# A decoder layer on one core: the attention phase's batch loop as a loop in hardware, and the head norm's means at another place

## The chip, the core and the metric

The kernel runs on one core of a Trainium2 chip. The metric is the device time of one execution in microseconds, median of three runs. A core has five instruction streams: TensorE (PE, with its weight loads PEld), VectorE (DVE), ScalarE (ACT), GpSimd (POOL) and SyncE (SP), which here issues the DMAs. They run in parallel and meet at semaphores only.

## The reference, cut to what matters

One decoder layer on x of 8 x 512 x 512, in three parts, each followed by a layer norm over the last axis without weights.

```python
x = _layernorm(x + attention(x, ...))        # the phase that the change is in
x = _layernorm(x + retention(x, ctx, ...))
x = _layernorm(x + coupling_network(x, ...))

# attention: 16 heads of 32
kv = _ln(x, kvn_w, kvn_b) @ kv_w + kv_b
q = _ln(x, qn_w, qn_b) @ q_w + q_b
q, k = _rotary(q, x, rh_w, rh_b), _rotary(k, x, rh_w, rh_b)
qn, kn = _ln(q, ln_w, ln_b), _ln(k, ln_w, ln_b)      # the head norm, over 32 elements
attn = softmax(einsum('bhqd,bhkd->bhqk', qn, kn) / sqrt(32))
out = einsum('bhqk,bhkd->bhqd', attn, v) @ out_w + out_b
```

## The kernel before

The three parts run one behind the other (`attention_phase`, `retention_phase`, `coupling_phase`). In the attention phase the work is cut into 32 units U = 4 b + g: b is one of 8 batch rows (B = 8), g one of four groups of four heads (G = 4, HG = 4). Each engine has its own list of instructions, written out by a function `unit(b, g, left, more)`: sixteen steps i = 0 to 15, and at each step the pieces that fall due there. `left` says how many units follow (4 for "enough"), `more` whether there is a batch row b + 2.

A unit works on several units' data at once. In unit U the engines do:

- for U: the key-side scores (`key_scores`, L929), their exponentials (`exps`, L796), the weighing of v (`weigh`, L939), the inverse of the sums, and at i = 15 the normalisation (`normalise`, L550); the high and low halves of its result are taken in the next unit (`attn_hi`, L802, `attn_low`, L554).
- for U + 1: the row scores (`query_scores`, L911) in three banks (NB = 3), so that product i waits for exponential i - 3; the row maxima (`row_max`, L526); their exponentials for the sums (`sum_exps`, L775); at the end the maxima are turned (`transpose_max`, L918), saved (`save_max`, L788) and spread (`spread_max`, L532).
- for U + 2: the head norm, for the key side (s = 0) and the query side (s = 1): mean on VectorE (`head_mean`, L497 and L499), subtraction on GpSimd (`centre`, L362), square on ScalarE (`square`, L759), variance on VectorE (`head_var`, L507 and L510), power and multiplications on GpSimd (`head_norm`, L368 to L377), transposes on TensorE (`turn_heads`, L897), halves, and 24 DMAs into `stack`.
- for U + 3: the projection (`project`, L886 to L888), its save by two additions (`save_qkv`, L489 and L491), and the rotation on GpSimd (`rotate`, L344 to L354), whose semaphore `turned` the mean waits for.
- with g = 0 also the output projection of the batch row before (L953 to L955), transposes of the next row's x, and only one bank for the projection.

The order on an engine is the order in which `unit` writes its pieces; an engine takes its instructions in that order. Tables at the head of the file set the steps: `QS_DONE`, `KS_DONE` and `PROJECT_DONE` say how many products are done after step i, `SQUARE_AT = (1, 2)` when ScalarE squares sides 0 and 1, `VAR_AFTER = (2, 3)` when VectorE takes the variances. Semaphores only count up, so that a wait names a number that grows with U. `steps` counts an engine's waits on its own operations. The class `Steps` has `loop` and `end`, and `in_registers` writes out the additions for a value that isn't a constant; neither is used before the change. `run` writes out all 32 units one behind the other for each engine.

Of the kernel before, what the change touches and what calls it, by code (L numbers as in the profile page):

```python
# [19 lines left out]
B, S, D = 8, 512, 512  # L20
T = S // P
K = D // P
H, HD = 16, 32
G = 4
HG = H // G
GQ = HG * HD
EPS = 1e-5

KS_DONE = tuple(min(4 * (i + 1) // 3, T * HG) for i in range(16))
QS_DONE = tuple(min(max(4 * (i - 1) // 3, 0), T * HG) for i in range(16))  # L30
# [4 lines left out]
Z_AT, Z_HIGH_AT, Z_LOW_AFTER = (12, 12, 13, 13), (13, 13, 14, 14), (13, 13, 14, 14)  # L35
MAX_AT, SAVE_MAX_AT = 14, 14
X_NORM_AT, STATS_AFTER, FINAL_AFTER, SHIFT_AFTER = (6, 7, 8, 9), (5, 7), 9, 4
VAR_AFTER, SQUARE_AT = (2, 3), (1, 2)
TURN_HIGH_AT, TURN_LOW_AFTER = ((9, 12), (9, 11)), ((10, 13), (10, 12))
INVERT_AFTER, INVERSE_AT, INVERSE_SAVE_AT, ATTN_HIGH_AT, ATTN_LOW_AFTER = 6, 11, 12, 0, 0  # L40
NB = 3
# [10 lines left out]
def in_registers(eng, *values):  # L52

    for value in values:
        if not isinstance(value, int):
            eng.compute_val(value)
# [78 lines left out]
def attention_phase(nc, x, x1, w, ctx_in, w_next, ret):  # L137
# [6 lines left out]
    with ctx:  # L144
# [87 lines left out]
        dve_step, pool_step = sem("dve_step"), sem("pool_step")  # L232
# [14 lines left out]

        block = ctx.enter_context(nc.Block())

        def run(unit):  # L250

            for b in range(B):
                for g in range(G):
                    unit(b, g, 4 if b < B - 1 else G - 1 - g, b + 2 < B)

        @block.sync
        def _(sp):
# [46 lines left out]
            for U in range(2):  # L304
                for s in range(2):
                    regroup_side(U, U, s)
            run(unit)
            sp.wait_ge(qkv_done, T * G * B)
            for m in (0, 2, 1):
                sp.dma_start(ret.raw[m], w_next[("Wk", "Wq", "Wv")[m]].rearrange("(k p) n -> p k n", p=P)).then_inc(ret.load_w, 16)  # L310
# [8 lines left out]
        def _(pool):  # L319
# [98 lines left out]
            x_rstd(1)  # L418
            for s in range(2):
                rotate(2, s)  # L420
            run(unit)
            pool.wait_ge(ret.xvar_done, 1)
            nc.gpsimd.tensor_tensor(ret.rstd[:, :], ret.rstd[:, :], minus_half[:, 0:T], ALU.pow).then_inc(ret.xrstd_done, 1)

# [1 line left out]
        def _(dve):  # L426
# [10 lines left out]
            def x_stats(b, t):  # L437

                if t == 0:
                    dve.wait_ge(x_in, 16 * (b + 1))  # L440
                nc.vector.bn_stats(stats[:, t, :], z[:, t, :])
                nc.vector.scalar_tensor_tensor(scratch[:, :], z[:, t, :], 1.0, rh_w[:, :], ALU.mult, ALU.mult,
                                               accum_out=per_step[:, t:t + 1]).then_inc(dve_step, 1)
                dve.wait_ge(dve_step, steps.next())

            def x_moments(b):

# [138 lines left out]
            def unit(b, g, left, more):  # L586
                U = G * b + g
                for i in range(T * HG):
                    if left == 0 and i == R_STATS_AT:
                        next_stats()  # L590
                    if left == 0 and i == R_NORM_AT:
                        next_norm()
                    if left == 0 and i in SPLIT_AT:
                        next_lower(*SPLITS[SPLIT_AT.index(i)])
                    if left >= 2 and i == 0:
                        for s in range(0 if U == 0 else 1, 2):
                            head_mean(U + 2, s)
                    if left >= 1:
                        for m in within(QS_DONE, i):
                            row_max(U + 1, m)  # L600
                    if left >= 3 and i in SAVE_AFTER[g > 0]:
                        t = SAVE_AFTER[g > 0].index(i)
                        save_qkv(U + 3, (g + 3) % G, t, bank_t[0 if g == 0 else t % 2])
                    if i == ATTN_LOW_AFTER and counts(U):
                        attn_low(U - 1, (g - 1) % G)
                    for s in range(2):
                        if left >= 2 and i == VAR_AFTER[s]:
                            head_var(U + 2, s, g == 2)
                    for s in range(2):
                        if left >= 2 and i == TURN_LOW_AFTER[g > 0][s]:  # L610
                            turn_low(U + 2, s, bank_t[s])
                    if g >= 2 and more and i in STATS_AFTER:
                        x_stats(b + 2, 2 * (g - 2) + STATS_AFTER.index(i))
                    if g == 3 and more and i == FINAL_AFTER:
                        x_final(b + 2)
                    if g == 0 and left == 4 and i == SHIFT_AFTER:
                        x_shift(b + 1)
                    for t in range(T):
                        if g == 0 and counts(b) and i == ADD_AFTER[t]:
                            add_out(b - 1, t, bank_t[1])  # L620
                        if g == 0 and left == 4 and i == Z_LOW_AFTER[t]:
                            z_low(b + 1, t)
                    if i == INVERT_AFTER:
                        invert(U, g % 2)
                    if i == SAVE_MAX_AT and left >= 3:
                        head_mean(U + 3, 0)
                    if i == SAVE_MAX_AT and left >= 1:
                        spread_max(U + 1, (g + 1) % 2)
                    if i == T * HG - 1:
                        normalise(U)  # L630
# [98 lines left out]
            spread_max(0, 0)  # L729
            for s in range(2):  # L730
                turn_low(1, s, bank_t[s])
            run(unit)
            attn_low(G * B - 1, G - 1)
            next_lower(*SPLITS[-2])
            for t in range(T):
# [4 lines left out]
        def _(act):  # L740
# [122 lines left out]
            save_max(0, 0)  # L863
            for s in range(2):
                turn_high(1, s, bank_t[s])
            run(unit)
            attn_hi(G * B - 1, G - 1)
            for m, half in SPLITS[-2:]:
                next_higher(m, half)
# [2 lines left out]
        def _(pe):  # L872
# [225 lines left out]
            for s in range(2):  # L1098
                pe.wait_ge(qkv_saved, T * 2 + 3 + s)
                turn_heads(1, s, bank_t[s])  # L1100
            run(unit)
            pe.wait_ge(attnT_done, G * B)
            for t in range(T):
                project_out_part(t, G - 1)
# [1066 lines left out]
```

## Time and profile before

| | |
|---|---|
| time, median of 3 runs | 2055.28 us (2052.32 to 2055.53) |
| the profiled execution's own time | 2052.32 us |
| its span, first to last instruction | 2050.4 us |
| instructions in it | 26478 |
| TensorE / weight loads busy | 1777.7 / 1329.2 us |
| VectorE / ScalarE / GpSimd busy | 1455.5 / 1258.5 / 861.0 us |
| mean granted TensorE clock | 0.946 of full |
| attention phase | the first 1097 us or so |

The span is what the trace covers; the own time is what is comparable with other runs. Busy times of engines overlap each other. A busy TensorE isn't TensorE at its peak, since its products are pipelined.

### The profile page before, as it was taken

How to read it: one execution, taken by the hardware profiler on the slowest of the kernel's cores; microseconds unless marked ns; L12 is line 12 of the kernel's file. 1: busy time of each engine (PE TensorE's matmuls, PEld its weight loads, DVE VectorE, ACT ScalarE, POOL GpSimd, SP SyncE). 2: the span in 40 equal slices, each digit the busy share in tenths (PEclk: the TensorE clock that was granted, in tenths of full speed). 3: DMA queues.
4: the chain of work that ended last, by engine and by line, in shares of the span. 5: the costliest groups of instructions: out<-in, count | busy, mean ns of one | idle time of the engine just before them, and what ended most of it. 6: DMA issues, size and time to landing. Idle time of an engine off the chain costs nothing. (4 is left out here: it accounts for less than half of the span.)

```text
span 2050.4 us, 26478 instructions
## 1 busy us (share of the span) xinstructions
PE 1777.7 (87%) x8648; PEld 1329.2 (65%) x8648; DVE 1455.5 (71%) x2915; ACT 1258.5 (61%) x2674; POOL 861.0 (42%) x802
## 2 busy tenths in 40 slices
PE   6788888888888888888888999999986999999972
PEld 5556566666566665666536878787775777777751
DVE  7768677686776867767655767676653678888876
ACT  3388777886868868688693232322323667777764
POOL 3677678676876768768521222222220000000000
PEclk9799999999999999999889999999997999999996
DMA  4222232322323223222252101111121011111111
GB/s 151 58 77 62 57 98 62 94 61 62 93 62 98 57 61 94 62 78 57 69 168 108 62 36 48 54 55 57 62 88 41 21 42 62 62 62 62 42 41 62
DMA packets 86184, 141.06 MB, mean 69 GB/s; under 512 B 16544, under 2 KB 19616, under 8 KB 86048
## 3 DMA queue, kind: packets, MB, share of 16 engines
q1 hardware_dynamic: 86048, 139.37, 22.0%
q8 instruction: 70, 1.15, 0.2%
q14 instruction: 66, 0.54, 0.1%
HBM read 63.82 MB, written 25.17 MB: 43 GB/s over the span
## 5 line engine op out<-in xcount | busy, mean ns | idle before, releaser
L526 DVE TENSOR_REDUCE a_neg_max<-a_max 128x1 fp32r<-128x512 f32 x512 | 340.4, 684 | 175.4 <-PE a_max L911 173.3
L796 ACT ACTIVATE a_probs<-a_exp 128x512 f32<-128x512 f32 x512 | 294.2, 606 | 209.6 <-PE a_exp L929 208.7
L775 ACT ACTIVATE a_max<-a_max,a_neg_max 128x512 f32<-128x512 f32 x512 | 347.1, 689 | 15.3 <-DVE a_neg_max L526 13.5
L911 PE MATMUL a_max<-a_stack 96*128 96x512 f32 x512 | 224.7, 463 | 92.3 <-ACT a_max L775 84.6
L368 POOL TENSOR_TENSOR a_rstd<-a_rstd,a_minus_half 128x16 f32<-128x16 f32 x64 | 186.0, 2906 | 90.4 <-DVE a_rstd L510 90.3
L911 PEld LDWEIGHTS a_max<-a_stack 96*128 96x128 f32 x512 | 99.1, 197 | 190.7 <-ACT a_max L775 141.0
L886 PE MATMUL a_t<-a_w_hi,a_zT_hi 128*128 128x384 f32 x500 | 181.5, 363 | 32.8 <-DVE a_v L491 23.0
L1717 POOL TENSOR_TENSOR f_yrstd<-f_yrstd,f_minus_half 128x4 f32<-128x4 f32 x8 | 11.0, 1376 | 472.0 <-DVE f_yrstd L1736 472.0
L929 PE MATMUL a_exp<-a_stack 100*128 100x512 f32 x512 | 192.0, 416 | 9.9 <-ACT a_probs L796 6.5
L887 PE MATMUL a_t<-a_w_lo,a_zT_hi 128*128 128x384 f32 x500 | 173.4, 347 | 0.0
L888 PE MATMUL a_t<-a_w_hi,a_zT_lo 128*128 128x384 f32 x500 | 173.2, 346 | 0.0
L939 PE MATMUL a_o<-a_probs,a_v 128*32 128x512 f32 x1024 | 151.1, 665 | 0.0
L886 PEld LDWEIGHTS a_t<-a_w_hi,a_zT_hi 128*128 128x128 f32 x500 | 99.3, 199 | 48.1 <-DVE a_v L491 31.3
L1449 ACT ACTIVATE r_kq_hi<-r_part 128x512 fp32r<-128x512 f32 x64 | 36.9, 625 | 147.3 <-POOL r_part L1316 147.3
L1996 PE MATMUL f_l<-f_h_hi,f_w_hi 128*128 128x512 f32 x240 | 100.6, 419 | 25.2 <-DVE f_h_lo L1726 24.6
L775 ACT ACTIVATION_READ_ACCUMULATOR a_max<-a_max,a_neg_max 128x1 f32 x512 | 120.4, 235 | 0.0
L929 PEld LDWEIGHTS a_exp<-a_stack 100*128 100x128 f32 x512 | 100.6, 197 | 28.6 <-ACT a_probs L796 15.7
L1996 PE MATMUL f_w<-f_xT_hi,f_w_hi 128*128 128x512 f32 x256 | 104.4, 408 | 7.4 <-DVE f_xT_lo L1726 7.4
L362 POOL TENSOR_TENSOR a_n<-a_n,a_mean 128x512 f32<-128x512 f32 x64 | 73.7, 1156 | 76.5 <-DVE a_mean L499 75.3
L887 PEld LDWEIGHTS a_t<-a_w_lo,a_zT_hi 128*128 128x128 f32 x500 | 99.5, 199 | 8.1
L1322 POOL TENSOR_TENSOR r_yrstd<-r_yrstd,r_minus_half 128x2 f32<-128x2 f32 x16 | 11.2, 697 | 222.8 <-DVE r_yrstd L1417 222.8
L1726 DVE TENSOR_TENSOR f_h_lo<-f_full,f_h_hi 128x512 fp32r<-128x512 f32 x104 | 70.4, 688 | 43.1 <-ACT f_h_hi L1899 42.0
(286 smaller groups left out, 4919.7 us busy)
## 6 DMA issues: line engine op xcount, KB each, us to landing
a_stack<-a_nT_hi SPq DMA_DIRECT2D x512, 64.0 KB, 2.0
a_stack<-a_nT_lo SPq DMA_DIRECT2D x256, 64.0 KB, 2.0
a_z<-x SPq DMA_DIRECT2D x8, 1024.0 KB, 7.9
a_y<-x SPq DMA_DIRECT2D x8, 1024.0 KB, 5.7
r_xn<-x SPq DMA_DIRECT2D x8, 1024.0 KB, 5.6
r_cn<-ctx SPq DMA_DIRECT2D x8, 1024.0 KB, 7.9
x<-r_xn SPq DMA_DIRECT2D x16, 512.0 KB, 2.8
f_xn<-x SPq DMA_DIRECT2D x8, 1024.0 KB, 5.6
```

What stands on the lines that cost most here:

```text
L362: nc.gpsimd.tensor_tensor(n[:, c], n[:, c], wide(mean[:, c]), ALU.subtract).then_inc(centred, 1)
L368: nc.gpsimd.tensor_tensor(rstd[:, c], rstd[:, c], minus_half[:, :], ALU.pow).then_inc(pool_step, 1)
L526: nc.vector.tensor_reduce(neg_max[:, t, ROW + h:ROW + h + 1].bitcast(F32R), bank_max[i % NB][:, :], AX_X, ALU.max, negate=True).then_inc(m ...
L775: nc.scalar.activation(bank_max[i % NB][:, :], bank_max[i % NB][:, :], ACT.Exp, bias=neg_max[:, t, ROW + h:ROW + h + 1], accum_out=sums[:, ...
L796: nc.scalar.activation(probs[:, kt % 2, h, :], bank_exp[i % 2][:, :], ACT.Exp).then_inc(exp_done, 1)
L886: mm(bank, zT_hi[:, k, at], w_hi[:, k, g, :], start=k == 0, stop=False)
L887: mm(bank, zT_hi[:, k, at], w_lo[:, k, g, :], start=False, stop=False)
L888: last = mm(bank, zT_lo[:, k, at], w_hi[:, k, g, :], start=False, stop=k == K - 1)
L911: mm(bank_max[i % NB][:, :], stack[0:ROW, par, h, t * P:(t + 1) * P], stack[0:ROW, par, HG + h, :], start=True, stop=True).then_inc(score_ ...
L929: mm(bank_exp[i % 2][:, :], stack[0:ROW + HG, par, HG + h, kt * P:(kt + 1) * P], stack[0:ROW + HG, par, h, :], start=True, stop=True).then ...
L939: last = mm(bank_o[at, :], v[:, g, kt, at], probs[:, kt % 2, h, :], start=kt == 0, stop=kt == T - 1, tile_position=(0, h * HD))
L1996: mm(bank, a_hi, b_hi, start=first, stop=False)
```

## The change

`run` no longer writes out all units. The first unit (b = 0, g = 0) stands alone; then each engine opens a loop of its own (`Fori`) with six passes, b = 0 to 5, each of which holds the units g = 1, 2, 3 of b and g = 0 of b + 1; the last seven units (b = 6 with g = 1 to 3, and b = 7) are written out again. In the loop b is a register, so that every semaphore value that depends on it is computed, and the addresses of the DMAs that depend on it too. GpSimd and VectorE say how many steps of their own they count in a pass (40 and 31).

The two means of the head norm for U + 2 are taken at the steps `MEAN_AFTER = (0, 1)` of unit U, behind the save of the projection and the low half. Before, side 1 was taken first of all at i = 0, and side 0 at i = 14 of the unit before (for U + 3 there). The variances move from steps 2, 3 to 3, 4. In `x_stats` the last of four steps computes its value first and has one wait more, on a semaphore that reached its value at the start.

```diff
--- before.py
+++ after.py
@@ -25,6 +25,8 @@
 HG = H // G
 GQ = HG * HD
 EPS = 1e-5
+DVE_STEPS, POOL_STEPS = 31, 40
+
 
 KS_DONE = tuple(min(4 * (i + 1) // 3, T * HG) for i in range(16))
 QS_DONE = tuple(min(max(4 * (i - 1) // 3, 0), T * HG) for i in range(16))
@@ -35,7 +37,7 @@
 Z_AT, Z_HIGH_AT, Z_LOW_AFTER = (12, 12, 13, 13), (13, 13, 14, 14), (13, 13, 14, 14)
 MAX_AT, SAVE_MAX_AT = 14, 14
 X_NORM_AT, STATS_AFTER, FINAL_AFTER, SHIFT_AFTER = (6, 7, 8, 9), (5, 7), 9, 4
-VAR_AFTER, SQUARE_AT = (2, 3), (1, 2)
+MEAN_AFTER, VAR_AFTER, SQUARE_AT = (0, 1), (3, 4), (1, 2)
 TURN_HIGH_AT, TURN_LOW_AFTER = ((9, 12), (9, 11)), ((10, 13), (10, 12))
 INVERT_AFTER, INVERSE_AT, INVERSE_SAVE_AT, ATTN_HIGH_AT, ATTN_LOW_AFTER = 6, 11, 12, 0, 0
 NB = 3
@@ -247,11 +249,22 @@
 
         block = ctx.enter_context(nc.Block())
 
-        def run(unit):
-
-            for b in range(B):
-                for g in range(G):
-                    unit(b, g, 4 if b < B - 1 else G - 1 - g, b + 2 < B)
+        def run(eng, unit, steps=None, per=0):
+
+
+            unit(0, 0, 4, False)
+            with eng.Fori(0, B - 2) as b:
+                if steps:
+                    steps.loop(b, per)
+                for g in range(1, G):
+                    unit(b, g, 4, True)
+                unit(b + 1, 0, 4, True)
+            if steps:
+                steps.end(B - 2)
+            for g in range(1, G):
+                unit(B - 2, g, 4, False)
+            for g in range(G):
+                unit(B - 1, g, G - 1 - g, False)
 
         @block.sync
         def _(sp):
@@ -304,7 +317,7 @@
             for U in range(2):
                 for s in range(2):
                     regroup_side(U, U, s)
-            run(unit)
+            run(sp, unit)
             sp.wait_ge(qkv_done, T * G * B)
             for m in (0, 2, 1):
                 sp.dma_start(ret.raw[m], w_next[("Wk", "Wq", "Wv")[m]].rearrange("(k p) n -> p k n", p=P)).then_inc(ret.load_w, 16)
@@ -418,7 +431,7 @@
             x_rstd(1)
             for s in range(2):
                 rotate(2, s)
-            run(unit)
+            run(pool, unit, steps, POOL_STEPS)
             pool.wait_ge(ret.xvar_done, 1)
             nc.gpsimd.tensor_tensor(ret.rstd[:, :], ret.rstd[:, :], minus_half[:, 0:T], ALU.pow).then_inc(ret.xrstd_done, 1)
 
@@ -441,7 +454,13 @@
                 nc.vector.bn_stats(stats[:, t, :], z[:, t, :])
                 nc.vector.scalar_tensor_tensor(scratch[:, :], z[:, t, :], 1.0, rh_w[:, :], ALU.mult, ALU.mult,
                                                accum_out=per_step[:, t:t + 1]).then_inc(dve_step, 1)
-                dve.wait_ge(dve_step, steps.next())
+                if t < T - 1:
+                    dve.wait_ge(dve_step, steps.next())
+                    return
+                step = steps.next()
+                in_registers(dve, step)
+                dve.wait_ge(split_done, 1)
+                dve.wait_ge(dve_step, step)
 
             def x_moments(b):
 
@@ -592,9 +611,6 @@
                         next_norm()
                     if left == 0 and i in SPLIT_AT:
                         next_lower(*SPLITS[SPLIT_AT.index(i)])
-                    if left >= 2 and i == 0:
-                        for s in range(0 if U == 0 else 1, 2):
-                            head_mean(U + 2, s)
                     if left >= 1:
                         for m in within(QS_DONE, i):
                             row_max(U + 1, m)
@@ -604,6 +620,8 @@
                     if i == ATTN_LOW_AFTER and counts(U):
                         attn_low(U - 1, (g - 1) % G)
                     for s in range(2):
+                        if left >= 2 and i == MEAN_AFTER[s]:
+                            head_mean(U + 2, s)
                         if left >= 2 and i == VAR_AFTER[s]:
                             head_var(U + 2, s, g == 2)
                     for s in range(2):
@@ -622,8 +640,6 @@
                             z_low(b + 1, t)
                     if i == INVERT_AFTER:
                         invert(U, g % 2)
-                    if i == SAVE_MAX_AT and left >= 3:
-                        head_mean(U + 3, 0)
                     if i == SAVE_MAX_AT and left >= 1:
                         spread_max(U + 1, (g + 1) % 2)
                     if i == T * HG - 1:
@@ -729,7 +745,7 @@
             spread_max(0, 0)
             for s in range(2):
                 turn_low(1, s, bank_t[s])
-            run(unit)
+            run(dve, unit, steps, DVE_STEPS)
             attn_low(G * B - 1, G - 1)
             next_lower(*SPLITS[-2])
             for t in range(T):
@@ -863,7 +879,7 @@
             save_max(0, 0)
             for s in range(2):
                 turn_high(1, s, bank_t[s])
-            run(unit)
+            run(act, unit)
             attn_hi(G * B - 1, G - 1)
             for m, half in SPLITS[-2:]:
                 next_higher(m, half)
@@ -1098,7 +1114,7 @@
             for s in range(2):
                 pe.wait_ge(qkv_saved, T * 2 + 3 + s)
                 turn_heads(1, s, bank_t[s])
-            run(unit)
+            run(pe, unit)
             pe.wait_ge(attnT_done, G * B)
             for t in range(T):
                 project_out_part(t, G - 1)
```

## Rows read from the trace of the kernel before

**Rows 1.** The page: the span, and the engines' busy time.

```profile
span 2050.4 us, 26478 instructions
...
PE 1777.7 (87%) x8648; PEld 1329.2 (65%) x8648; DVE 1455.5 (71%) x2915; ACT 1258.5 (61%) x2674; POOL 861.0 (42%) x802
```

**Rows 2.** Windows by unit: PE, PEld, DVE, ACT, POOL busy; clock, DMA, GB/s.

```profile
385.30:412.50 27.20, 24.06 (x133) 16.86 (x133) 20.86 (x40) 23.10 (x56) 22.07 (x21) 1.00 0.45 133
412.50:441.10 28.60, 24.98 (x130) 16.86 (x129) 23.92 (x47) 23.32 (x56) 23.75 (x22) 0.94 0.22 55
...
469.20:511.20 42.00, 37.33 (x195) 27.16 (x194) 24.84 (x48) 28.39 (x64) 24.81 (x24) 1.00 0.23 65
...
595.70:639.80 44.10, 37.57 (x189) 27.69 (x189) 25.32 (x49) 28.47 (x64) 24.17 (x23) 0.96 0.22 62
```

**Rows 3.** Waits, 120 to 1100 us: who for whom, us in total, times, longest.

```profile
PE a_max L911 <- ACT a_max L775: 77.1, 75, 1.6
...
DVE a_stack L532 <- ACT a_stack L788: 25.6, 21, 2.0
...
PE a_t L886 <- DVE a_v L491: 15.4, 14, 2.9
```

**Rows 4.** Timeline of the start of a unit with g = 2: start, duration, engine.

```profile
411.64 0.83 DVE L532 CAST a_stack<-a_stack 4x1024 fp32r<-4x1024 f32 x1 [0.85 <-ACT a_stack L788]
...
412.50 0.70 DVE L550 TENSOR_TENSOR a_o<-a_o,a_inverse 128x512 f32<-128x512 f32 x1
...
413.23 0.69 DVE L497 TENSOR_REDUCE a_mean<-a_n 128x16 f32<-128x512 f32 x1
...
413.53 0.59 ACT L802 ACTIVATE a_attnT_hi<-a_o 128x512 fp32r<-128x512 f32 x1
...
413.95 0.17 DVE L499 TENSOR_SCALAR a_mean<-a_mean 128x16 f32<-128x16 f32 x1
...
414.04 0.42 DVE L489 TENSOR_TENSOR a_qk<-a_t,a_qkv_bias 128x256 f32<-128x256 f32 x1
...
414.20 1.05 POOL L362 TENSOR_TENSOR a_n<-a_n,a_mean 128x512 f32<-128x512 f32 x1 [2.29 <-DVE a_mean L499]
...
415.31 0.60 ACT L796 ACTIVATE a_probs<-a_exp 128x512 f32<-128x512 f32 x1 [1.19 <-PE a_exp L929]
...
415.81 0.62 ACT L759 ACTIVATE a_turn<-a_n 128x512 f32<-128x512 f32 x1
...
417.28 0.64 ACT L759 ACTIVATE a_turn<-a_n 128x512 f32<-128x512 f32 x1
...
417.51 2.91 POOL L368 TENSOR_TENSOR a_rstd<-a_rstd,a_minus_half 128x16 f32<-128x16 f32 x1 [2.25 <-DVE a_rstd L510]
417.80 0.67 ACT L775 ACTIVATE a_max<-a_max,a_neg_max 128x512 f32<-128x512 f32 x1
...
418.64 0.50 PE L911 MATMUL a_max<-a_stack 96*128 96x512 f32 x1 [0.91 <-ACT a_max L775]
```

**Rows 5.** Timeline of the start of a unit with g = 0.

```profile
471.59 0.44 PE L886 MATMUL a_t<-a_w_hi,a_zT_hi 128*128 128x384 f32 x1 [0.99 <-DVE a_v L491]
```

**Rows 6.** Timeline of the head norm's end and its transposes.

```profile
427.03 1.28 POOL L377 TENSOR_TENSOR a_n<-a_n,a_head_b 128x512 f32<-128x512 f32 x1
...
427.34 0.60 PE L897 MATMUL a_t<-a_ident,a_n 128*128 128x128 f32 x4
...
432.89 1.12 PE L897 MATMUL a_t<-a_ident,a_n 128*128 128x128 f32 x4
```

**Rows 7.** DMA: queues (packets, MB, share) and issues (count, KB, us to landing).

```profile
q8 instruction: 70, 1.15, 0.2%
q14 instruction: 66, 0.54, 0.1%
...
a_stack<-a_nT_hi SPq DMA_DIRECT2D x512, 64.0 KB, 2.0
...
f_small<-L_ffn_gc_w SPq DMA_DIRECT2D x1, 0.5 KB, 5.3
```

## The prediction

> **What bounds the kernel now.** I read the totals of the page first. TensorE is busy 87% of the span, VectorE 71%, ScalarE 61%, GpSimd 42% [rows 1]: no engine is full, so the end is set by waits between engines. The chain that ended last doesn't reach back into the attention phase, so I read that phase, the only one the diff touches, by its units. A unit is one pass of the sixteen steps i = 0 to 15 for one group g of one batch row b. The windows of eight of them, cut where the softmax normalisation of one unit starts (line 550), show short units for g = 1, 2, 3 (27.2 and 28.6 us) and long ones for g = 0 (42.0 and 44.1 us). In the short ones TensorE is busy 24 to 25 us, ScalarE 23, VectorE 21 to 24, GpSimd 22 to 24 [rows 2]. So TensorE paces, with the three others a few us behind it.
>
> The table of waits in the phase says on whom TensorE waits: on ScalarE's exponential of the row scores (line 775) 77 us in 75 times, and on VectorE's save of the projections (line 491) 15 us [rows 3]. ScalarE's square (line 759) isn't among the waiters of that table. The timeline of the start of one unit (g = 2) shows where the first of TensorE's waits falls: the fourth score product starts at 418.64 after 0.91 us of waiting for the first exponential, which ScalarE had started at 417.80 [rows 4]. There are three score banks, so product 3 waits for exponential 0. The units behind it start in the same pattern. ScalarE comes to that exponential through its own queue: key exponential 1 at 415.31, square of side 0 at 415.81, two more key exponentials of 0.60 us, square of side 1 at 417.28, and then the row exponential at 417.80, with no idle time between [rows 4]. This stretch of ScalarE's queue is on the path of TensorE. That is what the reader should keep.
>
> **The change part by part.** It does three things: the means of the head norm move, 24 of the 32 units become six passes of a loop, with five jumps back on each engine, and waits in the loop compare with register values.
>
> *The means.* Before, the mean of side 0 is taken by VectorE at the end of a unit (i = 14), ahead of the spread of the maxima, for which VectorE then waits 0.85 us anyway; the mean of side 1 comes first in the next unit, 413.23 to 414.12. Both sides are centred by GpSimd (1.05 us each) well before ScalarE squares them at 415.81 and 417.28 [rows 4]. After, both means are taken in the next unit, side 0 at i = 0 behind the first projection save and the low half of the attention output, side 1 at i = 1 behind the second save. The two operations of a mean take 0.69 and 0.17 us, 0.89 with the gap; a save of the projections takes 0.42 for its first addition and some 0.65 in all. I follow them through the same unit, with the times of [rows 4]:
>
> Normalisation 412.50 to 413.20 as before. Save of t = 0 from 413.2 to 413.9 (0.8 earlier than before, the mean of side 1 is gone from ahead of it). Low half: waits for ScalarE's high half, which ends at 413.53 + 0.59 = 414.12, so 414.15 to 414.83. Mean of side 0: 414.83 to 415.72. Centre on GpSimd (1.05): 415.8 to 416.85. Square of side 0 on ScalarE: 416.9, where it was 415.81, and ScalarE has been free since 415.91. ScalarE takes its queue in order, so key exponentials 2 and 3 follow at 417.4 to 418.5. Meanwhile save of t = 1 to 416.4, mean of side 1 to 417.3, centre 417.35 to 418.4, square of side 1 418.45 to 419.05. Row exponential 0 at 419.0, where it was 417.80: 1.2 us late. The row maximum it needs (VectorE 417.3 to 418.0) is in time, so ScalarE is what is late. TensorE's fourth score product then starts at 419.85 instead of 418.64. TensorE waited there already, so the whole 1.2 us is on the path, and everything behind it in the unit shifts with it. The starts of the units g = 3 and g = 1 give the same by the same steps. Units with g other than 0 that still have a head norm to feed: 7 x 3 + 1 = 22. 22 x 1.2 = **+26.4 us**.
>
> For g = 0 the projection has one bank, and TensorE waits for the save itself: 0.99 us at 471.59, with the mean of side 1 ahead of the save [rows 5]. Without it TensorE could go on up to 0.9 us earlier; I take 0.5, since the save also waits for GpSimd's rotation of the unit before. The next projection and its save stand between the low half and the squares here, so the squares wait for nothing new, and row exponential 0 comes about 0.4 us earlier. 7 x 0.4 = **-2.8 us**.
>
> What is late next: the variances go from i = 2, 3 to 3, 4, so GpSimd's power starts at 419.6 instead of 417.51 [rows 4], 2.1 us late, 0.9 more than TensorE. The last product of the chain is there at 428.31 and TensorE's transposes that need it start at 432.89 [rows 6], so 4.6 us of slack cover it: nothing. The end of the unit: VectorE is free 0.9 us earlier, but the spread of the maxima waits for ScalarE (25.6 us in 21 of the phase's 31 units [rows 3]): nothing, with at most 10 x 0.9 = 9 us of gain as the other bound. The added wait on a semaphore that is long satisfied (x_stats, t = 3, six times) I cost at nothing.
>
> *The jumps.* Five times each engine goes back to the head of the loop. The trace shows no jump of this kind. The page says that instructions arrive by DMA: 70 and 66 packets, 1.15 and 0.54 MB, which is 1.69 MB for 26478 instructions, 64 bytes each, so each is fetched once and in order [rows 1, 7]. A pass of four units has some 3 x 130 + 195 = 585 matrix products on TensorE [rows 2], with a weight load each, so its head must be fetched again if it isn't kept. Lower bound 0: kept, or covered by work in the queues. Upper bound: the smallest load, of 0.5 KB, lands 5.3 us after its issue; the 64 KB loads land after 2.0 us [rows 7]. At the unit's end TensorE has the four transposes of the maxima (four such take 0.60 us [rows 6]) and then nothing queued but the next unit, so little covers a fetch. I take 2.5 us a jump, nearer the 2.0 row: 5 x 2.5 = **+12.5 us** (0 to 26.5).
>
> The Trainium skill, "Runtime: NRT & Kernel Launch", section "Instruction fetch mechanics", says that prefetch is purely sequential and that a taken branch whose target is outside the current window forces a DMA fetch before execution goes on. It speaks against the change; by it the jump term is paid, by a reading in which loops are free it is 0 and the sum is 12.5 us less. No row here shows which.
>
> *The registers.* By the code, a unit on TensorE has about 55 waits (19 of the score products, 19 of the key products, 5 at the weighing, 12 others); in 24 units 1320, each with a value that must first be added up in a register. Nearest row: four transposes with four weight loads take 0.60 us, 0.075 us an instruction [rows 6]. If each register operation stood on the path: 1320 x 0.075 = 99 us. If the queues run ahead: 0; TensorE's waits are on ScalarE and VectorE [rows 3], so while it waits its queue can fill. I take two exposed ones a unit (a wait behind another wait): 24 x 2 x 0.075 = **+3.6 us**.
>
> The Trainium skill, "Advanced Engine Details and Errata", section "Sequencer Loop", says that an engine instruction waits for its semaphore in a queue while the sequencer reads on, which is the reading I chose.
>
> *TensorE's clock.* Two units g = 0 with the same work took 42.0 us at a granted clock of 1.00 and 44.1 at 0.96; of the eight windows five lie under 1.00, and two of these stand in [rows 2]. A drop to 1.2 GHz costs up to 2.1 us. Longer waits at the units' starts make more of them. Bounds: none more, or one in each of the 3/8 of 32 units that had none, 12 x 2.1 = 25. I take three: **+6.3 us**.
>
> Sum: 26.4 - 2.8 + 12.5 + 3.6 + 6.3 = 46.0. The profiled execution took 2052.3 us (span 2050.4 and 1.9 around it), so 2098.3. The median of the three runs shown is 2055.3, 3.0 higher, so the forecast for the median is **2101 us**, +2.2%.
>
> **The rivals.**
> *Jumps and registers free, means as computed*: 26.4 - 2.8 = 23.6, so 2079. For it: waits leave time to fill queues. Against: little is queued at the unit's end.
> *More clock drops*: TensorE's wait at each short unit's start grows from 0.91 to 2.1 us, and the clock falls in most units: 46 - 6.3 + 25 = 65, so 2120; with the jumps at 5.3 us 2134. For it: five of eight units already have a drop. Against: the units' starts also have the densest work.
> *Registers on the path*: two thirds of the 99 us: 2055 + 42 + 66 = 2163. For it: TensorE's weights follow each other closely. Against: its waits are on other engines.
> *No change*: the late squares are absorbed, which needs ScalarE 1.2 us ahead at its first row exponential, and free jumps: 2055. Against: the 0.91 us wait.
> *Faster*: the mean at a unit's end holds the spread of the maxima in the 10 of 31 units where that doesn't wait for ScalarE (at most 9 us), and g = 0 gives 2.8: 2055.3 - 11.8 = 2043.5. It decides if the centred side 0 is there when ScalarE is free at 415.91, that is, if the mean is done by 414.8; I get 415.7.
>
> **How the numbers follow.** Forecast as summed 0.56, jumps and registers free 0.14, more clock drops 0.10, registers on the path 0.07, no change 0.06, faster 0.07. Faster by over 0.2% (4 us, about what a measurement of this kernel can tell from no change) 0.07, within 0.2% 0.06, slower by over 0.2% 0.87. The range leaves out the registers on the path, no change and faster, 0.20: from 2062 (the free case, with part of the squares absorbed) to 2138 (clock drops with dear jumps).
>
> **What would show it.** In the trace after: ScalarE's square (line 759 before) waits on GpSimd's centring in short units, near 1 us each, some 20 us in total; TensorE's wait on the row exponential grows by a like amount; the short units inside and outside the loop are both about 1.2 us longer; units with g = 0 aren't. Jumps: at five places, all behind a unit with g = 0, idle time on several engines at once that "issue" ends; instruction DMA per executed instruction shows whether the head is fetched again. Registers: short units in the loop longer than those behind it (b = 6). I am wrong if the square doesn't wait, if the loop's units grow by several us that no wait on the means explains, or if the unit ends get shorter by 1 us.

## The result, and the profile after

The changed kernel took 2084.5 us (median of 4 runs, 2077.6 to 2087.8) where the kernel before took 2055.4 (4 runs, 2052.3 to 2055.6) on the same chip: ratio 1.013, with a 95% interval of 1.0109 to 1.0151, so 1.3% slower. All 13 executions of it on record lie between 2075.1 and 2087.8, with a median of 2081.3. A second comparison (below) gave 1.0120 (1.0095 to 1.0144), by medians 21.7 us where the first has 29.1. The profiled execution took 2075.1 us, 22.8 over that of before. The forecast was 2101, with a range of 2062 to 2138.

The page of the changed kernel: span, busy time and the two instruction queues. Lines of the code moved: GpSimd's by 13, VectorE's by 19, ScalarE's and TensorE's by 16.

```profile
span 2073.3 us, 29038 instructions
...
PE 1785.2 (86%) x8648; PEld 1334.4 (64%) x8648; DVE 1456.7 (70%) x2915; ACT 1263.1 (61%) x2674; POOL 857.6 (41%) x802
...
q8 instruction: 47, 0.77, 0.2%
q14 instruction: 67, 0.55, 0.1%
```

The work is the same as in [rows 1]. Queue q8 fetched 23 packets and 0.38 MB less than in [rows 7], q14 the same. The windows by unit, with the columns of [rows 2] (two units with g = 1 and 2, two with g = 0):

```profile
390.40:420.60 30.20, 26.54 (x137) 18.97 (x137) 20.00 (x39) 23.32 (x56) 21.30 (x20) 0.94 0.41 120
420.60:450.10 29.50, 25.28 (x129) 16.93 (x129) 23.02 (x47) 23.55 (x56) 23.57 (x22) 0.94 0.22 54
481.60:522.10 40.50, 35.16 (x184) 25.29 (x184) 25.52 (x50) 28.54 (x64) 23.69 (x22) 1.00 0.23 65
612.50:653.60 41.10, 35.62 (x186) 25.45 (x185) 25.87 (x49) 28.43 (x64) 25.06 (x24) 1.00 0.23 65
```

Against [rows 2] the short units are longer (30.2 and 29.5 us for 27.2 and 28.6), and the long ones shorter (40.5 and 41.1 for 42.0 and 44.1). The waits of the phase (120 to 1100 us), first the one line of before that [rows 3] doesn't hold, then the kernel after:

```profile
PE a_exp L929 <- ACT a_probs L796: 5.8, 22, 0.8
```

```profile
PE a_max L927 <- ACT a_max L791: 79.4, 75, 1.6
DVE a_stack L551 <- ACT a_stack L804: 45.5, 24, 2.8
...
ACT a_turn L775 <- POOL a_n L375: 23.3, 22, 2.2
PE a_exp L945 <- ACT a_probs L812: 21.6, 34, 1.4
PE a_t L902 <- DVE a_v L510: 11.6, 14, 1.6
```

ScalarE's square (line 775) now waits for GpSimd's centring, 22 times and 23.3 us. TensorE's wait for the row exponential hardly grew (77.1 to 79.4); its wait for the key exponential did (5.8 to 21.6). The timeline of the unit that stands in [rows 4] shows both:

```profile
423.00 0.68 DVE L516 TENSOR_REDUCE a_mean<-a_n 128x16 f32<-128x512 f32 x1
...
423.97 1.05 POOL L375 TENSOR_TENSOR a_n<-a_n,a_mean 128x512 f32<-128x512 f32 x1 [5.26 <-DVE a_mean L518]
...
425.06 0.63 ACT L775 ACTIVATE a_turn<-a_n 128x512 f32<-128x512 f32 x1 [0.90 <-POOL a_n L375]
...
425.59 1.07 ACT L812 ACTIVATE a_probs<-a_exp 128x512 f32<-128x512 f32 x2
...
426.22 0.50 PE L945 MATMUL a_exp<-a_stack 100*128 100x512 f32 x1 [0.71 <-ACT a_probs L812]
...
427.07 0.66 ACT L791 ACTIVATE a_max<-a_max,a_neg_max 128x512 f32<-128x512 f32 x1
...
427.90 0.50 PE L927 MATMUL a_max<-a_stack 96*128 96x512 f32 x1 [0.93 <-ACT a_max L791]
```

From the normalisation at 420.61 the square of side 0 is 4.45 us away, where it was 3.31 (415.81 from 412.50), and the row exponential 6.46, where it was 5.30 (417.80): 1.16 us late. The 0.71 us that TensorE waits at 426.22 for a key exponential, queued behind the square, is most of it; the wait at the fourth score product keeps its 0.93.

### The profile page after: what moved, and what is told of

It reads as the page before. It is cut to its first block and busy times, and to the rows that moved or that the text cites. A ratio compares the mean times of both kernels' runs of the same rounds, so it can differ in the third digit from the quotient of the medians.

```text
span 2073.3 us, 29038 instructions
## 1 busy us (share of the span) xinstructions
PE 1785.2 (86%) x8648; PEld 1334.4 (64%) x8648; DVE 1456.7 (70%) x2915; ACT 1263.1 (61%) x2674; POOL 857.6 (41%) x802
## 5 line engine op out<-in xcount | busy, mean ns | idle before, releaser
L945 PE MATMUL a_exp<-a_stack 100*128 100x512 f32 x512 | 196.7, 425 | 25.6 <-ACT a_probs L812 22.3
L955 PE MATMUL a_o<-a_probs,a_v 128*32 128x512 f32 x1024 | 146.0, 644 | 0.0
L375 POOL TENSOR_TENSOR a_n<-a_n,a_mean 128x512 f32<-128x512 f32 x64 | 67.2, 1050 | 153.7 <-DVE a_mean L518 153.2
L2014 PE MATMUL f_w<-f_xT_lo,f_w_hi 128*128 128x512 f32 x256 | 100.6, 393 | 0.0
```

The lines of the kernel that those rows point to most:

```text
L945: mm(bank_exp[i % 2][:, :], stack[0:ROW + HG, par, HG + h, kt * P:(kt + 1) * P], stack[0:ROW + HG, par, h, :], start=True, stop=True).then ...
L955: last = mm(bank_o[at, :], v[:, g, kt, at], probs[:, kt % 2, h, :], start=kt == 0, stop=kt == T - 1, tile_position=(0, h * HD))
L2014: return mm(bank, a_hi, b_lo, start=False, stop=last)
```

## The experiments

Mean unit lengths in the trace, from one normalisation's start to the next, over the 24 units that the loop covers (six of each g); in brackets the part up to row exponential 0. They show where each kernel's time lies:

| kernel | g = 1 | g = 2 | g = 3 | g = 0 |
|---|---|---|---|---|
| before | 27.54 (5.95) | 28.93 (5.79) | 28.05 (5.25) | 43.07 (9.05) |
| after | 29.62 (7.79) | 30.28 (6.54) | 31.08 (6.29) | 40.85 (7.49) |
| after_again | 29.54 (7.78) | 30.41 (6.64) | 30.05 (6.39) | 40.74 (7.38) |
| after_once | 30.00 (7.79) | 30.37 (6.47) | 29.96 (6.10) | 40.73 (7.37) |
| means_only | 30.59 (7.79) | 30.33 (6.90) | 28.00 (6.35) | 40.98 (7.79) |
| short_only | 30.05 (7.79) | 29.62 (6.62) | 29.22 (6.39) | 43.61 (10.40) |
| mixed | 27.56 (5.96) | 29.09 (5.75) | 28.03 (5.19) | 41.40 (7.37) |
| means_sq | 28.41 (6.76) | 28.21 (6.21) | 27.95 (5.23) | 41.08 (7.87) |
| mixed_sq | 27.48 (5.96) | 28.68 (6.30) | 27.87 (5.73) | 41.79 (7.79) |
| loop_only | 29.07 (7.49) | 28.46 (5.70) | 27.43 (5.28) | 43.21 (9.07) |
| loop_once | 27.57 (6.03) | 28.71 (5.84) | 27.76 (5.30) | 43.27 (9.12) |

### The parts by themselves (one chip; the kernel before 2055.9 us, 23 runs)

**means_only**: unrolled as before, with the new places alone.

```diff
-VAR_AFTER, SQUARE_AT = (2, 3), (1, 2)
+MEAN_AFTER, VAR_AFTER, SQUARE_AT = (0, 1), (3, 4), (1, 2)
...
```

> All 32 units written out as before, with the two means and the variances at their new places. If the late squares are what costs (the forecast's means term), this alone takes 2055 + 20 to 25 = 2075 to 2080 us, with ScalarE's square waiting some 20 us on the centring and the units with g = 0 shorter than before. If the loop is what costs and the means are absorbed, it takes 2053 to 2058 us.

Measured: 2066.5 us, ratio 1.0056 (1.0041 to 1.0071), +10.5. By the table the short units give 6 x (3.05 + 1.40 - 0.05) = +26.4 us, and the long ones 6 x -2.09 = -12.5; these 13.9 and the 10.5 of the times differ by what lies outside the 24 units and by noise. The places of the means are two effects of opposite sign, both large.

**loop_only** is the loop with the old places. **loop_once** is the same with the loop written out as six loops of one pass, so that the registers stay and no engine jumps back:

```diff
-            with eng.Fori(0, B - 2) as b:
+            for once in range(B - 2):
+                most = 1 if eng.engine == mybir.EngineType.SP and once == B - 3 else 2
+                with eng.Fori(once, once + most, most) as b:
...
```

> The loop of six passes, with means and variances at the places they had before. If the means are what costs, 2055 + 3 to 8 = 2058 to 2063 us. If jumps cost 2.5 us each and registers 3.6 us, as forecast, 2071 us. If the loop makes the whole difference, 2080 to 2086 us.

> As the loop with the old places, but written out six times with one pass each: the same register operations and register waits, and no jump back. What it takes less than the loop with the old places is the price of five jumps (forecast 12.5 us; if TensorE keeps the loop's instructions and the others' queues cover theirs, under 2 us). What it takes more than before is the price of the registers (forecast 3.6 us; rival 10 us and more).

Measured: loop_only 2059.4 us, ratio 1.0023 (1.0004 to 1.0042); loop_once 2059.2, ratio 1.0018 (1.0007 to 1.0029). The registers cost about 3 us, and the jumps nothing that the times tell; the two intervals leave room for up to some 5 us. The trace of loop_only does show them, on VectorE. Its waits in the phase, the timeline at one jump, and its queue on the page:

```profile
DVE a_mean L516 <- issue: 14.5, 5, 3.0
```

```profile
386.65 0.70 DVE L569 TENSOR_TENSOR a_o<-a_o,a_inverse 128x512 f32<-128x512 f32 x1
390.26 0.69 DVE L516 TENSOR_REDUCE a_mean<-a_n 128x16 f32<-128x512 f32 x1 [2.91 <-issue]
...
391.87 0.45 PE L905 MATMUL a_t<-a_w_hi,a_zT_hi 128*128 128x384 f32 x1 [1.48 <-DVE a_v L510]
```

```profile
q14 instruction: 92, 0.75, 0.1%
```

Five times, once a jump, VectorE stands for 2.9 us and nothing that the profile shows ends it; TensorE passes 1.5 us of it on, and the g = 1 units are 1.5 us longer than in loop_once (29.07 and 27.57). The other short units are a little shorter, so that all 24 units together take 5.2 us more than in loop_once's trace, which is of its fastest execution. Queue q14 has 25 packets more than in the kernel after. TensorE and ScalarE don't stand at a jump.

**after_once** has the new places and the registers, without jumps back (the edit of loop_once on the changed kernel).

> The changed kernel, but with its loop written out six times with one pass each: new places, registers, no jump back. With jumps at 2.5 us it is 12.5 us faster than the changed kernel (2084), at 2072; with jumps free it is within 2 us of it. If the changed kernel's wide spread of times (10 us) comes from fetching instructions behind jumps, it is gone here.

Measured: 2072.9 us, ratio 1.0079 (1.0061 to 1.0097). That is 6.4 over means_only and 11.6 under the changed kernel's time, which comes from another comparison; the next set has both on one chip. Its times spread over 11 us (2068.2 to 2079.3), as those of the changed kernel do over some 13, so the spread isn't gone without the jumps.

### The jumps again, and the long units alone (one chip; before 2055.3 us, 11 runs)

**after_again** is the changed kernel, **after_once_again** after_once, and **after_dve_once** has only VectorE's loop written out:

```diff
-            with eng.Fori(0, B - 2) as b:
+            once_here = eng.engine in (mybir.EngineType.DVE,)
+            for once in range(B - 2 if once_here else 1):
+                first, last, step = (once, once + 2, 2) if once_here else (0, B - 2, 1)
+                with eng.Fori(first, last, step) as b:
...
```

> The changed kernel once more, so that it stands on the same chip as the next two. It was 29 us over the kernel before in its own comparison, and the same kernel without the jumps back 17 us over it in another: between 2080 and 2088 us if the places of the means (some +10), the registers (some 0) and the jumps back add up. Theory A: the five jumps back cost 8 to 14 us here, 2 to 3 us each, so this run lies that much above the next. Rival: the 12 us between the two were the difference of two comparisons and the real cost of a jump is under 1 us each; then this run lies within 5 us of the next.

> The changed kernel with its loop written out six times as loops of one pass: the registers stay, no engine ever jumps back. Theory A: 2070 to 2076 us, 8 to 14 below the changed kernel. Rival: 2076 to 2084, within 5 us of it.

> The changed kernel with VectorE's loop alone written out as six loops of one pass; TensorE, ScalarE, GpSimd and SyncE keep their loop with the jump back. Theory A: the jump costs on VectorE, which stood still for 2.9 us after it where the loop was made alone; this run equals the one without any jump (within 3 us of it). Theory B: what the jumps cost is on ScalarE, GpSimd or TensorE; this run equals the changed kernel, 8 to 14 us above the one without any jump. If the jumps cost nothing all three are equal.

Measured: 2077.0, 2075.8 and 2076.6 us; ratios 1.0120 (1.0095 to 1.0144), 1.0096 (1.0080 to 1.0113), 1.0096 (1.0079 to 1.0114). The times don't bear out theory A (8 to 14 us): the three medians lie within 1.2 us and the intervals overlap. By the medians the five jumps cost the changed kernel 1.2 us, by the ratios 4.9; one of after_again's six times is 2090.3, which moves the ratio and not the median. The intervals leave room for up to some 11 us, but the traces show nothing of it: the g = 1 units, which stand behind the jumps, are no longer with them (29.62 and 29.54) than without (30.00). In the changed kernel's trace VectorE's only wait that "issue" ends in the phase is this, at no jump:

```profile
DVE a_neg_max L545 <- issue: 0.4, 1, 0.4
```

**mixed**: unrolled, the new places in the units with g = 0 alone.

```diff
-VAR_AFTER, SQUARE_AT = (2, 3), (1, 2)
+MEAN_AFTER, VAR_AFTER, SQUARE_AT = (0, 1), ((2, 3), (3, 4)), (1, 2)
...
-                    if left >= 2 and i == 0:
-                        for s in range(0 if U == 0 else 1, 2):
-                            head_mean(U + 2, s)
+                    if left >= 2 and i == 0 and g > 0:
+                        head_mean(U + 2, 1)
...
+                        if left >= 2 and g == 0 and i == MEAN_AFTER[s]:
+                            head_mean(U + 2, s)
-                        if left >= 2 and i == VAR_AFTER[s]:
+                        if left >= 2 and i == VAR_AFTER[g == 0][s]:
...
-                    if i == SAVE_MAX_AT and left >= 3:
+                    if i == SAVE_MAX_AT and left >= 3 and g < G - 1:
```

> The kernel before, unrolled, with the new places of the means and variances only in the units with g = 0, whose starts were 1.3 us shorter in the changed kernel and whose whole length was 2.1 us shorter; the other 24 units keep the old places. Theory: the g = 0 units gain without the others losing, 7 times 1.3 to 2.1 us, so 2041 to 2048 us. Rival: the gain of the g = 0 units was bought by what the units before them do (the side of a mean that the old order takes at the end of the unit before), or TensorE's clock takes it back in the next unit; then within 0.2% of the kernel before, 2052 to 2060 us.

Measured: 2035.3 us (4 runs, 2034.9 to 2042.9), ratio 0.9906 (0.9891 to 0.9920), 20 us faster than before and the fastest of all. The long units are 1.7 us shorter each, the short ones as before. That is 10 to 12 us of the 20: the profiled execution was the slowest of the four (2042.9, the others 2034.9 to 2035.4), so no trace shows where the other 8 lie. The start of the same long unit, before and in mixed, tells why:

```profile
595.08 2.94 POOL L382 TENSOR_TENSOR a_y<-a_y,a_out_bias 128x512 f32<-128x512 f32 x2
...
596.43 0.69 DVE L497 TENSOR_REDUCE a_mean<-a_n 128x16 f32<-128x512 f32 x1
...
597.15 0.90 DVE L499 TENSOR_SCALAR a_mean<-a_mean 128x16 f32<-128x16 f32 x1
597.96 0.41 DVE L489 TENSOR_TENSOR a_qk<-a_t,a_qkv_bias 128x256 f32<-128x256 f32 x1
...
598.63 0.69 PE L886 MATMUL a_t<-a_w_hi,a_zT_hi 128*128 128x384 f32 x1 [2.85 <-DVE a_v L491]
```

```profile
597.94 0.42 DVE L489 TENSOR_TENSOR a_qk<-a_t,a_qkv_bias 128x256 f32<-128x256 f32 x1 [0.45 <-PE a_t L889]
...
598.62 0.44 PE L887 MATMUL a_t<-a_w_hi,a_zT_hi 128*128 128x384 f32 x1 [0.49 <-DVE a_v L491]
...
599.95 0.68 DVE L497 TENSOR_REDUCE a_mean<-a_n 128x16 f32<-128x512 f32 x1
600.66 0.17 DVE L499 TENSOR_SCALAR a_mean<-a_mean 128x16 f32<-128x16 f32 x1
```

Before, the mean stands ahead of the save, its small scaling takes 0.90 us beside GpSimd's bias addition, and TensorE waits 2.85 us. At the end of that wait its clock falls to 1.2 GHz (before, a window of that stretch, its clock the third number from the end):

```profile
598.60:602.30 3.70, 3.67 (x12) 3.67 (x13) 0.57 (x1) 0.00 (x0) 1.43 (x2) 0.55 0.42 103
```

In mixed the save is first and TensorE waits 0.49 (so in three of the six long units, 1.35 to 1.64 in the others); no unit with g = 0 has a clock drop at all, where before three of them had.

### Short units alone, the square, and the loop with better places (one chip; before 2052.7 us, 13 runs)

**short_only** is mixed turned round: `g > 0` for `g == 0`, and the side-0 mean at the unit's end kept for g = 3 alone.

> The kernel before, unrolled, with the new places of the means and variances in the units with g = 1, 2 and 3 alone; the units with g = 0 keep the old places. The counterpart of the kernel with the new places in g = 0 alone, which ran 20 us under the kernel before, while both together ran 10.5 over it. If the two parts add, this one runs about 10.5 + 20 = 30 us over the kernel before, 2085 us (2080 to 2091): the late centring and square cost the 22 to 24 short units 1.2 to 1.3 us each. Rival: the two parts do not add (TensorE's clock answers to the whole), and this runs within 15 us of the kernel before, 2060 to 2070.

Measured: 2085.0 us, ratio 1.0165 (1.0146 to 1.0184), +32.4. The parts add: -20.0 + 32.4 = +12.4, for the 10.5 measured together. The short units are 6 x (2.51 + 0.69 + 1.17) = 26.2 us longer in the trace; the rest is in the long ones (+3.2) and outside the 24 units.

**means_sq**: means_only with the squares one step later, behind the first row exponentials.

```diff
-MEAN_AFTER, VAR_AFTER, SQUARE_AT = (0, 1), (3, 4), (1, 2)
+MEAN_AFTER, VAR_AFTER, SQUARE_AT = (0, 1), (3, 4), (2, 3)
...
```

> The unrolled kernel with all new places (10.5 us over the kernel before) and ScalarE's two squares one step later, behind the first row exponentials instead of ahead of them. Theory: the late mean costs through the square that waits for its centring ahead of row exponential 0 in ScalarE's queue; with the squares out of its way the short units start as before, and the time falls to 2030 to 2045 us, 20 to 35 below the kernel with all new places. Rival: VectorE itself is what is late (two reductions more ahead of the row maxima, which the exponentials need), or the late squares hold the variances, on which VectorE waits ahead of the row maxima; then it stays within 10 us of the kernel with all new places, 2056 to 2076.

Measured: 2039.6 us, ratio 0.9934 (0.9918 to 0.9949): from 10.5 over the kernel before to 13.1 under it. The means stand as late as in means_only; only the waiting square has left ScalarE's way. The short units are back to the length of before (by the table +0.3 us in 18), and the long ones keep their gain. TensorE's wait for the key exponential, in means_only and then in means_sq:

```profile
PE a_exp L926 <- ACT a_probs L793: 19.3, 26, 1.3
```

```profile
PE a_exp L926 <- ACT a_probs L793: 2.5, 4, 0.8
```

By the two ratios the step is worth 25 us. So the late mean cost through the square's place in the queue, not through VectorE's load. Part of the 25 us came by TensorE's clock: over units 1 to 27 it was at 1.2 GHz for 38 us in means_sq's trace and for 55 in that of means_only.

**mixed_sq**: mixed with the squares at (2, 3) and all variances at (3, 4).

> The kernel with the new places in g = 0 alone (20 us under the kernel before), and the squares one step later and the variances behind row maxima 3 and 4 in every unit. Where the squares stand ahead of row exponential 0 they take 1.3 us of ScalarE, and TensorE's fourth score product waits 0.9 us for that exponential in most units. If that is on the path, this runs up to 20 us under the kernel with the new places in g = 0 alone: 2015 to 2030 us. If the delay only moves to a later exponential, or the later variances hold GpSimd, it is within 5 us of it or slower: 2033 to 2050.

Measured: 2041.1 us, ratio 0.9942 (0.9929 to 0.9955): faster than before, not than mixed. The key exponential's wait is gone here too (2.2 us in 4 times, for 6.8 in mixed), but VectorE's variance reduction waits 13.2 us in 28 times for the squares (1.9 in mixed), ahead of the row maxima. So where the means are early in the short units, the square's later place, here together with later variances, gains nothing; where they are late it gives 25 us.

**loop_mixed**: the changed kernel's loop with mixed's places.

> The loop of the changed kernel with the new places in g = 0 alone. If the loop costs with these places what it cost with the old ones (3 to 4 us), this runs at 2037 to 2042 us, under the kernel before. If the loop costs what it did with the new places everywhere (10 to 18 us), 2046 to 2054.

Measured: 2042.2 us, ratio 0.9954 (0.9938 to 0.9971), 10.5 under the kernel before. The median lies at the end of my first range. But mixed's ratio, from another chip, is 0.0048 lower (10 us), more than the 3.5 us of loop_only, as in my second; this too is part of what stays open below. VectorE's waits in it have none that "issue" ends, although the unit behind a jump begins as in loop_only, with the mean of side 1.

## Why the prediction was right, and where it wasn't

The direction, the place and the likeliest case's main term held; the sum came out 46.0 for 22 to 29 measured (the two pairs of medians; 25 and 27 by the ratios), above all through two terms, both too high: the long units and the jumps. The number on record that came nearest was the rival of free jumps and registers, 2079, with a chance of 0.14. That it came so near is in part luck, since it has the long units' term as small as the sum has. By its own steps:

- **What bounds the kernel**: right. A queue of ScalarE's ahead of the row exponential was on TensorE's path: taking the square out of it gave 25 us (means_sq against means_only).
- **The means in short units, +26.4**: right in size. Short_only and means_only show +26.2 and +26.4 for the 18 in the 24 units, 1.5 us each where I had 22 times 1.2. The stepwise times held to 0.1 us (row exponential 1.16 us late for 1.2). Evenly spread it was not: the g = 1 units start 1.84 us late, the others 0.75 to 1.1. And the wait that grew is the one before: TensorE meets the key exponential first, behind the square in the same queue. I had named the row exponential as what would show it.
- **g = 0, -2.8**: this step failed in size: -12.5 us over six units in means_only's trace and -20 us in mixed's time. I took one unit's wait of 0.99 us [rows 5] for all. Three of the six in the table had 2.67 to 2.85, all with a clock drop at their end (one window of [rows 2], 44.1 us at 0.96, is such a unit), and I allowed 0.5 of the 0.9 us that the mean held the save. Of the 20 us a trace shows 10 to 12.
- **The jumps, +12.5**: wrong, 1 to 5 by medians and ratios, with room up to 11. In the changed kernel nothing waits at a jump. Where one did cost (loop_only) it was on VectorE, 2.9 us, near the 2.5 that I took, and 1.5 reached TensorE.
- **The registers, +3.6**: right with the old places (+3.2, interval 1.4 to 6.0). With the new ones 6.4 by the medians (after_once over means_only), 4.7 by the ratios.
- **TensorE's clock, +6.3**: about right. Summed from windows of 1 us over units 1 to 27, before had 61 us at 1.2 GHz, after 75 and in the second trace 68; at half speed these 7 to 14 us are 3 to 7 lost. But the long units lost their drops and the g = 3 units gained them, which no step of mine had, so the size is right by luck.
- **Units behind the loop** (b = 6): g = 1 is 2.1 us longer, g = 2 and 3 aren't (27.48 and 27.17 for 27.39 and 28.24), so of 22 short units 19 paid in the changed kernel. In means_only the g = 3 units don't pay either, and the other twelve pay more.
- The end of the unit, 0 with at most 9 us of gain: in the long units the part from the transposes of the maxima to the normalisation fell from 3.08 us (before, mixed) to 2.27 (means_only), 4.9 us in six; in the short ones it didn't. The variances moved as computed: GpSimd's power starts 7.13 us behind the normalisation in the unit followed, where it started at 5.01. No trace shows a cost of that.

Measured parts: 26.4 for short units, -12.5 for long ones, 3.2 for registers, 1 to 5 for jumps, so 18 to 22 of the 22 to 29. What stays open is whether registers and new places together cost more than apart, and why. The times of one chip don't show it: by the ratios means_only and loop_once add up to 0.0074, and after_once has 0.0079. The traces do (the 24 units take 6.9 us more in after_once than in means_only, where loop_once's are 1.7 us under before), and they give a place, not a cause: in after, after_again and both runs without jumps some g = 3 units have a clock drop of 6.8 us early on, in means_only none has. The same unit in after and in means_only, in windows:

```profile
714.40:720.00 5.60, 4.20 (x22) 3.52 (x21) 5.45 (x13) 2.93 (x7) 2.10 (x2) 1.00 0.43 105
720.00:726.80 6.80, 5.86 (x18) 5.24 (x17) 4.75 (x11) 4.31 (x12) 5.24 (x3) 0.54 0.36 87
```

```profile
711.35:716.95 5.60, 4.27 (x23) 3.58 (x21) 5.49 (x13) 3.00 (x7) 2.10 (x2) 1.00 0.43 105
716.95:723.75 6.80, 5.87 (x32) 4.17 (x31) 5.73 (x13) 5.95 (x16) 5.93 (x3) 1.00 0.36 87
```

The first 5.6 us differ by 0.07 us of TensorE's work, the next 6.8 by 14 products. What tips the clock I can't say from these.

## What to carry to other kernels

Ask of a moved operation which in-order queue its consumer stands in, and what stands behind it there: moving the consumer by one step gave back 25 us, about what the late mean had cost the short units. Size a term from all units of its kind, the worst first, and where units differ, try the edit on each kind alone; here one edit was +32 us in one kind and -20 in the other. A loop may cost next to nothing, but look at the first instructions behind the jump on every engine.

## What the runs showed of the hardware

- **A jump's cost depends on the engine and the program.** VectorE stood 2.9 us at each jump in loop_only and not in after or loop_mixed, with 92 packets on q14 there for 67 and 68. The queue says whether the head was fetched again. With VectorE's loop alone written out (after_dve_once) q14 has 80 packets and 0.66 MB, with all loops written out 81: so VectorE's pass was kept in after (67, 0.55 MB), and in loop_only (92, 0.75 MB) it was fetched anew, five packets more a jump. TensorE never stood; q8 has 0.77 MB with the loop and 1.18 with it written out (after_once), 0.41 MB less, by my estimate five passes of some 1280 instructions at 64 bytes, so it fetched its pass once. The Trainium skill, "Runtime: NRT & Kernel Launch", section "Instruction fetch mechanics", gives TensorE room for 2048 instructions and the others 512, with blocks of 256. If the window of its rule on taken branches is that room, TensorE's pass is inside it and the rule doesn't bite; the trace agrees. I had used the rule and passed over the sizes. VectorE's pass, by the 0.11 MB some 340 instructions, is under its 512 too, and loop_only fetched it again all the same. That the head's place in its block decides for VectorE would fit both outcomes, but no run here tests it.
- **VectorE's small operations stretch beside GpSimd.** The mean's scaling took 0.90 us for 0.17, and ended with the bias additions beside it (598.05 and 598.02); the spread of the maxima took up to 1.73 us for 0.69 beside the same additions (the kernel before, at 185.75). The Trainium skill, "SBUF — State Buffer", section "SBUF: two separate sides", says that some VectorE operations and GpSimd's hold a port pair for a whole instruction and exclude each other; this trace agrees for these.
- **TensorE's clock was at 1.2 GHz** for 3.4 us each, from the end of its waits of 2.7 to 2.9 us in three long units of before. In mixed, where it waited 0.5 to 1.6 us at these places, it stayed at 2.4. Such a wait isn't enough by itself: in loop_only TensorE waited 2.65 to 2.66 us in three long units, in short_only 2.72 in two, and its clock stayed at 2.4 there.
